# Key-key and key-query products of a chunked delta rule as pairs on two column halves of TensorE, in a new order of the step

## The chip, the cores and the metric

One core of one Trainium2 chip runs the whole kernel. The metric is the device time of one launch in microseconds (us), lower is better. The engines are TensorE (PE; its weight loads are listed apart as PEld), VectorE (DVE), ScalarE (ACT), GpSimd (POOL) and SyncE (SP), which issues most of the DMAs.

## The reference

Everything is float32. Two batches of 2048 tokens with 128 features go through a delta-rule attention with 4 heads and then through a mixture of 8 experts.

```python
q = (x @ Wq).reshape(b, n, H, DK)          # H = 4, DK = 128, DV = 32
k = (x @ Wk).reshape(b, n, H, DK)          # then k /= |k|, q *= DK ** -0.5
v = (x @ Wv).reshape(b, n, H, DV)
beta = sigmoid(x @ Wb)
def step(S, inp):                           # over the n = 2048 tokens
    q_t, k_t, v_t, b_t = inp
    pred = einsum('bhk,bhkv->bhv', k_t, S)
    delta = (v_t - pred) * b_t[..., None]
    S = S + k_t[..., :, None] * delta[..., None, :]
    o_t = einsum('bhk,bhkv->bhv', q_t, S)
    return (S, o_t)
o = o * rsqrt(mean(o * o) + EPS) * norm_w * (g * sigmoid(g))
x = layernorm(x + o @ Wo)
# then: top-2 of 8 experts with a capacity, silu(x @ w1) * (x @ w3) @ w2, weighted sum, layernorm
```

## The kernel before, in words

The attention works on chunks of P = 128 tokens. There are NP = 16 chunks in each of the B = 2 batches, and both batches go through together, so a step of the outer loop handles chunk p of both, in U = 8 units of (batch, head). Keys and queries are never formed. With Mk = Wk Wk^T and Nq = Wk Wq^T for each head, `keys` makes y = Mk x and `queries` makes gq = Nq x, and then two products with x itself give what the chunk needs:

- `key_key(n, b)`: x^T y for the 4 heads of one batch, a matrix of 128 x 512 (4 heads of 128 x 128) in one bank of PSUM. ACT copies it out (`key_key_out`, to `A`). It is symmetric for each head, and what is read of it later is the blocks of 32 x 32 on the diagonal, and of the rest those below the diagonal.
- `key_query(n, b)`: x^T gq, 128 x 512 as well. DVE multiplies it with an upper triangle (`masked`, to `PT`), so that of the lower left quarter of each head nothing is left.

In the profile, the first is the line with `ps<-y,xTs` and the second `ps<-gq,xTs`. A float32 product shows in the trace as two MATMUL records with their weight loads.

The inverse of the chunk's triangular matrix is made in stages, from blocks of 16 (solved on POOL, `solve`) to 32 (`z_32`, `w_32`), to 64 (`z_64`, `w_64`) and to 128 (`z_128`, `w_128`). These are many small products on parts of TensorE's array, and between each two stages stands a copy on DVE or ACT: `z64_copy` (DVE) is between `z_64` and `w_64`, `t64_copy` (DVE) between `w_64` and `z_128`, `z128_copy` (ACT) between `z_128` and `w_128`, `t128_copy` (ACT) between `w_128` and `deltas`. Beside this runs the state: `state_keys`, `keys_read` (DVE), `turn_keys`, `residues` (DVE), `deltas`, `deltas_out` (ACT), `turn_deltas`, `deltas_turned` (ACT), `new_state` and `outputs`. Behind the outputs come `head_sums`, `head_norms` (ACT), `gated_values` and `gated_out` (DVE), `project`, `normalise`, `experts`, `place`, and on POOL `scatter`, which writes rows to the expert slots with four DMA_INDIRECT for each chunk.

All these stages stand in one loop `for p in range(NP + LAST)` on each engine, in an order written out by hand; `at(what, n)` runs a stage if chunk n exists, and chunks at different stages are in work at once. Each engine takes its instructions in program order and waits on semaphores. Three banks of PSUM (0 to 2) go round among the big products: `STEP_FILLS` lists the 10 fills of a step with the chunk that each is for, and fill i takes bank i % 3, so it waits until fill i - 3 has been copied out (`free_bank`). `LV` is the bank of the inverse, `CB` that of the turned tiles, `ZA` the state, `OB` the outputs, `MB` the projection. `apart(eng)` issues a nop ahead of a group. From chunk 5 on, `products` uses a split of both operands into float32r parts, which shows as the lines L684, L685 and L686.

After the attention comes the expert part, in which TensorE, ACT and DVE work on 16 half-experts of 640 slots each; the change doesn't touch it. `keep_on` issues products that nobody reads.

## Time and profile before

| | |
|---|---|
| three runs | 532.18, 538.74, 542.06 us; median 538.74 |
| span of the profiled execution | 539.8 us |
| PE busy | 489.4 us, 91% of the span |
| DVE, ACT, POOL busy | 330.4, 325.2, 325.4 us |
| mean granted clock of TensorE | 0.955 of full speed |

The profiled execution's own time is its span of 539.8 us from first to last instruction, within the three runs. Busy time is the union of an engine's instructions; since the ends of matmuls are modelled and each overlaps the next, a busy PE may still be waiting for a little. The distance from the start of one group to the start of the next is the better measure of what a group costs.

### The profile page before, as it was taken

The numbers are of one execution on the slowest core, as the hardware profiler recorded it, in microseconds if no ns is written. First come the engines' busy times: TensorE is split into PE (matmuls) and PEld (weight loads), VectorE is DVE, ScalarE is ACT, GpSimd is POOL, SyncE is SP. The second block draws the span as 40 slices with busy tenths as digits, with TensorE's granted clock in tenths as the row PEclk, the third lists the DMA queues.
The fourth block names the chain that finished last, engine by engine and source line by source line (L and its number), as shares of the span: only waits on it lengthen the run. The fifth ranks groups of instructions, "written<-read, shape, count | busy, mean of one in ns | idle before, by whom it ended". The sixth has DMA issues, their size and how long they took to land.

```text
span 539.8 us, 18897 instructions
## 1 busy us (share of the span) xinstructions
PE 489.4 (91%) x7053; PEld 403.7 (75%) x7053; DVE 330.4 (61%) x1321; ACT 325.2 (60%) x905; POOL 325.4 (60%) x445
## 2 busy tenths in 40 slices
PE   6979989999999999999997887999999999999910
PEld 4666767767777777676765577999999999999910
DVE  4436558758778686776876762556445565455445
ACT  2645767777768877677664632555555555555454
POOL 3053717867678676786764542376667776767662
PEclk9998999999999999999988878999999999999965
DMA  3358664672554735547183223254536545453367
GB/s 93 31 85 224 215 149 46 94 106 26 73 47 57 101 35 72 49 58 95 24 174 36 32 31 103 36 109 56 109 56 127 110 57 107 60 123 35 30 129 213
DMA packets 154804, 46.09 MB, mean 85 GB/s; under 512 B 107168, under 2 KB 149280, under 8 KB 154720
## 3 DMA queue, kind: packets, MB, share of 16 engines
q1 hardware_dynamic: 132848, 29.86, 28.5%
q0 software_dynamic: 20288, 9.51, 18.9%
q10 hardware_dynamic: 1584, 5.59, 2.7%
q8 instruction: 54, 0.88, 0.7%
q14 instruction: 30, 0.25, 0.1%
HBM read 21.39 MB, written 23.55 MB: 83 GB/s over the span
## 4 chain that ended last, share of the span: by engine, by line
PE 73%; DMA 7%; DVE 7%; issue 6%; ACT 2%; SPq 2%; POOL 1%; ACTq 0%; DVEq 0%; POOLq 0%
PE ps L986 16%; PE ps L997 10%; PE ps L724 5%; PE ps L709 4%; PE ps L681 3%; PE ps L768 2%; PE ps L684 2%; PE ps L758 2%; PE ps L876 2%; PE ps L748 2%; PE ps L850 2%; PE ps L1012 2%; PE ps L780 2%; PE ps L738 2%; PE ps L685 2%
## 5 line engine op out<-in xcount | busy, mean ns | idle before, releaser
L1771 POOL DMA_INDIRECT x_store<-xk,row x80 | 125.1, 1563 | 68.8 <-ACT xk L1258 49.3
L1730 POOL DMA_INDIRECT slots_in<-x,slot x64 | 99.4, 1553 | 29.3 <-issue 17.8
L1589 DVE TENSOR_TENSOR hb<-ps,hs 128x320 f32<-128x320 f32 (+1 forms) x128 | 62.6, 492 | 51.0 <-ACT hs L1250 47.4
L1250 ACT ACTIVATE hs<-ps 128x320 f32<-128x320 f32 (+1 forms) x128 | 55.4, 435 | 34.5 <-PE ps L986 28.9
L986 PE MATMUL ps<-xeTh,w13h 128*128 128x320 f32 x224 | 71.2, 318 | 1.4 <-DVE xeTl L1613 1.0
L986 PE MATMUL ps<-xeTl,w13h 128*128 128x320 f32 x224 | 69.8, 312 | 0.0
L986 PE MATMUL ps<-xeTh,w13l 128*128 128x320 f32 x224 | 69.8, 311 | 0.0
L997 PE MATMUL ps<-w2s,hb 128*128 128x128 f32 x512 | 64.8, 279 | 1.0 <-DVE hb L1589 0.6
L997 PEld LDWEIGHTS ps<-w2s,hb 128*128 128x128 f32 x512 | 59.9, 192 | 3.5 <-DVE hb L1589 1.5
L1712 POOL TENSOR_TENSOR prod<-a,xs 128x28 f32<-128x28 f32 (+11 forms) x120 | 32.7, 272 | 31.5 <-DVE xs L1422 22.8
L1258 ACT ACTIVATE xk<-ps,gs 128x128 f32<-128x128 f32 x80 | 24.2, 365 | 44.5 <-PE ps L1012 34.9
L986 PEld LDWEIGHTS ps<-xeTh,w13h 128*128 128x128 f32 x224 | 42.7, 191 | 1.8 <-issue 1.3
L986 PEld LDWEIGHTS ps<-xeTl,w13h 128*128 128x128 f32 x224 | 42.7, 191 | 0.0
L986 PEld LDWEIGHTS ps<-xeTh,w13l 128*128 128x128 f32 x224 | 42.7, 191 | 0.0
L1744 POOL TENSOR_TENSOR Vk<-V,sq 128x256 f32<-128x256 f32 x16 | 10.7, 671 | 51.4 <-ACT sq L1091 51.3
L1713 POOL TENSOR_TENSOR xs<-xs,prod 128x28 f32<-128x28 f32 (+11 forms) x120 | 33.8, 281 | 9.4
L724 PE MATMUL ps<-gq,xTs 128*128 128x512 f32 x64 | 36.5, 655 | 0.0
L1108 ACT ACTIVATE TT<-x32T 32x256 f32<-32x256 f32 x64 | 26.5, 414 | 15.5 <-DVE x L1364 14.9
L709 PE MATMUL ps<-y,xTs 128*128 128x512 f32 x64 | 34.0, 621 | 1.8 <-ACT eg L1079 1.1
L684 PE MATMUL ps<-xeTh,w13h 128*128 128x256 f32 x99 | 33.3, 337 | 0.0
L1066 ACT ACTIVATE hb<-ps 128x512 f32<-128x512 f32 x32 | 19.1, 597 | 17.9 <-PE ps L709 12.6
L685 PE MATMUL ps<-xeTl,w13h 128*128 128x256 f32 x99 | 27.9, 282 | 0.0
(210 smaller groups left out, 1109.3 us busy)
## 6 DMA issues: line engine op xcount, KB each, us to landing
slots_in<-zeros ACTq DMA_DIRECT2D x10, 520.0 KB, 5.3
xe<-slots_in SPq DMA_DIRECT2D x15, 325.0 KB
w<-w_in SPq DMA_DIRECT2D x8, 448.0 KB
xTs<-xT SPq DMA_DIRECT2D x4, 512.0 KB, 4.9
a_diag<-hb SPq DMA_DIRECT2D x64, 32.0 KB
inv<-xs SPq DMA_DIRECT2D x16, 128.0 KB
xi<-inv SPq DMA_DIRECT2D x16, 128.0 KB
xk<-x SPq DMA_DIRECT2D x8, 256.0 KB, 5.2
```

The source lines that it names most:

```text
L684: mm(to, hi, xhs[:, r], start=True, stop=False)
L685: mm(to, hi, xls[:, r], start=False, stop=False)
L709: mm(ps[:, to, :], xTs[:, b, cols(n)], y[:, n % YR, b].rearrange("p h t -> p (h t)"), start=True, stop=True).then_inc(fill_mm, 1)
L724: mm(ps[:, to, :], xTs[:, b, cols(n)], gq[:, n % 2, b].rearrange("p h t -> p (h t)"), start=True, stop=True).then_inc(fill_mm, 1)
L986: last = mm(ps[:, HB[fill % 5], 0:HALF], w_[:, P * c:P * c + P], x_[:, par, cols], start=(t == 0), stop=(t == 2))
L997: last = mm(result_at(i), hb[:, par, c, P * i:P * i + P], w2s[:, we, c, :], start=(first and c == 0), stop=(stop and c == chunks[-1]), ski ...
L1250: af(hs[to, s % 4, :], ps[src, HB[fill_of(s) % 5], 0:HALF], ACT.Silu).then_inc(hs_ready, 1)
L1589: v.tensor_tensor(hb[to, par, c, HALF * g:HALF * g + HALF], ps[rows_, at, 0:HALF], hs[rows_, s % 4, :], ALU.mult).then_inc(h_ready, 1)
L1712: link(g.tensor_tensor(pr_, bc(a16[r, j + 1:, j], 2, j + 1), bc(xs[r, 0, j, 0:j + 1], 1, m), ALU.mult))
L1713: link(g.tensor_tensor(xs[r, 0, j + 1:, 0:j + 1], xs[r, 0, j + 1:, 0:j + 1], pr_, ALU.subtract))
L1730: g.indirect_dma_start(out=xs_d[:, :], out_offset=bass.IndirectOffsetOnAxis(ap=to, axis=0), in_=x1[:, p % 2, j, k, :], in_offset=None, com ...
L1771: g.indirect_dma_start(out=x1_d[:, :], in_=ye[:, par, i, :], in_offset=None, out_offset=bass.IndirectOffsetOnAxis(ap=row[:, par, i:i + 1], ...
```

## The change

Each 512-column product is cut into two. The array is used as two halves of 64 columns: one half of the output's rows is made with all 512 moving columns, the other half with only the 4 x 64 moving columns of the quarters that are still wanted, so that one quarter of the 128 x 512 result (in each head a block of 64 x 64) is no longer written. For key-key the rows 64 to 127 are whole and the rows 0 to 63 get columns 0 to 63 of each head; for key-query it is the other way about. `key_pair(n, m, b)` issues the products of chunk n (key-key) and of chunk m (key-query) alternately, so that neighbours lie on different column halves. Where only one of the two chunks exists (the first and last steps), only its two products are issued.

The fills' order, and with it the order of the stages on TensorE, ACT and DVE, is another. SP and POOL keep theirs.

```diff
-STEP_FILLS = (("v", 1, 0), ("kk", 1, 0), ("kq", 5, 1), ("g", 4, 0), ("gq", 4, 0), ("gq", 4, 1), ("kk", 1, 1),
-              ("y", 0, 0), ("kq", 4, 0), ("y", 0, 1))
+STEP_FILLS = (("kk", 1, 0), ("kq", 5, 0), ("gq", 4, 0), ("g", 4, 0), ("kk", 1, 1), ("kq", 5, 1), ("gq", 4, 1),
+              ("y", 0, 0), ("y", 0, 1), ("v", 0, 0))
...
+            def key_pair(n, m, b):
+
+                kk, kq = 0 <= n < NP, 0 <= m < NP
+                if kk:
+                    pe.wait_ge(y_free, 2 * n + 2)
+                    to_k = free_bank("kk", n, b)
+                    kT = xTs[:, b, cols(n)]
+                    ys = y[:, n % YR, b]
+                if kq:
+                    pe.wait_ge(gq_out, 2 * m + 2)
+                    to_q = free_bank("kq", m, b)
+                    qT = xTs[:, b, cols(m)]
+                    gs_ = gq[:, m % 2, b]
+                apart(pe)
+                if kk:
+                    mm(ps[64:128, to_k, :], kT[:, 64:128], ys.rearrange("p h t -> p (h t)"), start=True, stop=True)
+                if kq:
+                    mm(ps[0:64, to_q, :], qT[:, 0:64], gs_.rearrange("p h t -> p (h t)"), start=True, stop=True)
+                if kk:
+                    mm(ps[0:64, to_k, :].rearrange("p (h t) -> p h t", h=H)[:, :, 0:64], kT[:, 0:64], ys[:, :, 0:64],
+                       start=True, stop=True).then_inc(fill_mm, 1)
+                if kq:
+                    mm(ps[64:128, to_q, :].rearrange("p (h t) -> p h t", h=H)[:, :, 64:128], qT[:, 64:128],
+                       gs_[:, :, 64:128], start=True, stop=True).then_inc(fill_mm, 1)
...
             for p in range(NP + LAST):
-                at(values, p - 1)
                 at(turn_keys, p - 5)
-                at(key_key, p - 1, 0)
+                at(project, p - 6)
                 at(z_128, p - 5)
-                at(project, p - 6)
...
-                at(key_query, p - 5, 1)
+                key_pair(p - 1, p - 5, 0)
                 at(w_128, p - 5)
+                at(queries, p - 4, 0)
                 at(gate_in, p - 4)
-                at(queries, p - 4, 0)
                 at(deltas, p - 5)
+                key_pair(p - 1, p - 5, 1)
                 at(state_queries, p - 5)
+                at(turn_deltas, p - 5)
                 at(queries, p - 4, 1)
-                at(turn_deltas, p - 5)
-                at(key_key, p - 1, 1)
...
-                at(key_query, p - 4, 0)
+                at(head_sums, p - 5)
+                at(keys, p, 1)
                 at(z_64, p - 4)
                 at(state_keys, p - 4)
-                at(head_sums, p - 5)
-                at(keys, p, 1)
+                at(values, p)
                 at(w_64, p - 4)
```

On TensorE, from `w_64` (`ps<-z,x 32x32`) to `w_128` (`ps<-z,x 64x64`), with `turn_keys` (`ps<-ident,KSt`), `project` (`ps<-wox,og`) and `z_128` (`ps<-TT,hb`) between them, there stands before:

```order
L768 MATMUL ps<-z,x 32x32 x16
L703 MATMUL ps<-wvb,xTs 128x132 x2
L813 MATMUL ps<-ident,KSt 128x128 x2
L709 MATMUL ps<-y,xTs 128x512
L780 MATMUL ps<-TT,hb 64x64 x8
L882 MATMUL ps<-wox,og 128x136 x2
L724 MATMUL ps<-gq,xTs 128x512
L792 MATMUL ps<-z,x 64x64 x8
```

and now, begun two groups earlier at `z_64` (`ps<-x32T,hb`) and `state_keys` (`ps<-y,Zs`):

```order
L771 MATMUL ps<-x32T,hb 32x32 x16
L819 MATMUL ps<-y,Zs 32x128 x8
L703 MATMUL ps<-wvb,xTs 128x132 x2
L781 MATMUL ps<-z,x 32x32 x16
L826 MATMUL ps<-ident,KSt 128x128 x2
L895 MATMUL ps<-wox,og 128x136 x2
L793 MATMUL ps<-TT,hb 64x64 x8
L730 MATMUL ps<-y,xTs 64x512
L732 MATMUL ps<-gq,xTs 64x512
L734 MATMUL ps<-y,xTs 64x4x64
L737 MATMUL ps<-gq,xTs 64x4x64
L805 MATMUL ps<-z,x 64x64 x8
```

The product `ps<-y,xTs` has moved from ahead of `z_128` to behind it, `project` from behind to ahead, and `values` (`ps<-wvb,xTs`) from behind `w_64` to ahead of it; `head_sums` and the second `keys`, which stood between `state_keys` and `w_64`, are now ahead of `z_64`.

On TensorE from `deltas` (`ps<-TT,R`) to `turn_deltas` (`ps<-ident,dT`) and on to `count`, before:

```order
L822 MATMUL ps<-TT,R 32x128 x8
L838 MATMUL ps<-gq,Zs 32x128 x8
L684 MATMUL ps<-xeTh,w13h 128x256
L685 MATMUL ps<-xeTl,w13h 128x256
L686 MATMUL ps<-xeTh,w13l 128x256
...
L829 MATMUL ps<-ident,dT 128x128 x2
L709 MATMUL ps<-y,xTs 128x512
```

and now:

```order
L835 MATMUL ps<-TT,R 32x128 x8
L730 MATMUL ps<-y,xTs 64x512
L732 MATMUL ps<-gq,xTs 64x512
L734 MATMUL ps<-y,xTs 64x4x64
L737 MATMUL ps<-gq,xTs 64x4x64
L851 MATMUL ps<-gq,Zs 32x128 x8
L842 MATMUL ps<-ident,dT 128x128 x2
```

The second pair stands between two groups of the same form (`deltas` and `state_queries`) that were neighbours.

On DVE from the end of `x32_copy` to `x_rest`, before:

```order
L1364 STREAM_TRANSPOSE x<-x32T 128x256
L1405 COPY Zs<-ps 128x256
L1438 TENSOR_TENSOR PT<-ps,upper 128x512
L1371 COPY z<-ps 32x256 x2
L1394 COPY KSt<-ps 128x256
L1445 TENSOR_TENSOR osl<-o,silu 128x256
L1380 TENSOR_SCALAR TT<-ps 32x8x32 x2
L1450 TENSOR_TENSOR og<-osl,orms 128x256
L1389 STREAM_TRANSPOSE x<-TT 32x32 x8
L1400 TENSOR_TENSOR R<-Vk,ps 128x256
L1532 TENSOR_TENSOR xeTl<-xTs,xeTh 128x256
```

and now:

```order
L1374 STREAM_TRANSPOSE x<-x32T 128x256
L1415 COPY Zs<-ps 128x256
L1381 COPY z<-ps 32x256 x2
L1404 COPY KSt<-ps 128x256
L1455 TENSOR_TENSOR osl<-o,silu 128x256
L1460 TENSOR_TENSOR og<-osl,orms 128x256
L1390 TENSOR_SCALAR TT<-ps 32x8x32 x2
L1399 STREAM_TRANSPOSE x<-TT 32x32 x8
L1410 TENSOR_TENSOR R<-Vk,ps 128x256
L1542 TENSOR_TENSOR xeTl<-xTs,xeTh 128x256
L1448 TENSOR_TENSOR PT<-ps,upper 128x512
```

`masked` (`PT<-ps,upper`) left this stretch for one behind `x_rest`, and `gated_out` (`og`) moved ahead of `t64_copy` (`TT<-ps`). On ACT, `z128_copy` now comes ahead of the first `key_key_out`, `x1_rstd` comes behind `gate_out`, and `gate_sigmoid`, `key_norms` and `t_diag` come later, `t_diag` behind `head_norms`.

## Rows read from the trace of the kernel before

**Rows 1.** The page: busy time of TensorE, and the chain that ended last.

```profile
PE 489.4 (91%) x7053; PEld 403.7 (75%) x7053; DVE 330.4 (61%) x1321; ACT 325.2 (60%) x905; POOL 325.4 (60%) x445
...
PE 73%; DMA 7%; DVE 7%; issue 6%; ACT 2%; SPq 2%; POOL 1%; ACTq 0%; DVEq 0%; POOLq 0%
```

**Rows 2.** Busy time in a stretch (start:end, length, engines, granted clock); `turn_keys` from 100 to 240 us.

```profile
140.00:180.00 40.00, 39.55 (x829) 29.53 (x829) 28.63 (x126) 30.33 (x91) 27.52 (x45) 1.00 0.54 68
...
L813 PE MATMUL ps<-ident,KSt x18: 272/272/273, 100.7 to 238.3; 128*128 128x128 f32 x18
```

**Rows 3.** Timeline of TensorE over one step: start, busy us, line, names, forms.

```profile
135.41 0.38 PE L813 MATMUL ps<-ident,KSt 128*128 128x128 f32 x2
135.62 1.02 PE L709 MATMUL ps<-y,xTs 128*128 128x512 f32 x2
136.58 0.68 PE L780 MATMUL ps<-TT,hb 64*64 64x64 f32 x16
137.19 0.73 PE L882 MATMUL ps<-wox,og 128*128 128x136 f32 x4
137.76 1.02 PE L724 MATMUL ps<-gq,xTs 128*128 128x512 f32 x2
138.75 0.68 PE L792 MATMUL ps<-z,x 64*64 64x64 f32 x16
...
140.62 0.64 PE L822 MATMUL ps<-TT,R 128*32 128x128 f32 x16
141.08 0.62 PE L838 MATMUL ps<-gq,Zs 128*32 128x128 f32 x16
...
142.67 1.02 PE L709 MATMUL ps<-y,xTs 128*128 128x512 f32 x2
143.53 0.17 PE L889 MATMUL ps<-M,rest 128*128 128x16 bf16 x1
...
147.46 1.02 PE L724 MATMUL ps<-gq,xTs 128*128 128x512 f32 x2
148.41 0.69 PE L758 MATMUL ps<-x32T,hb 32*32 32x32 f32 x32
149.04 0.77 PE L806 MATMUL ps<-y,Zs 128*32 128x128 f32 x16
...
151.07 0.69 PE L768 MATMUL ps<-z,x 32*32 32x32 f32 x32
151.69 0.72 PE L703 MATMUL ps<-wvb,xTs 128*128 128x132 f32 x4
152.25 0.38 PE L813 MATMUL ps<-ident,KSt 128*128 128x128 f32 x2
```

**Rows 4.** Timeline of the three engines around `z64_copy` and `t64_copy`.

```profile
149.56 0.85 DVE L1371 COPY z<-ps 32x256 f32<-32x256 f32 x2 [0.34 <-PE ps L758]
...
150.43 0.43 DVE L1394 COPY KSt<-ps 128x256 f32<-128x256 f32 x1
150.78 0.41 DVE L1445 TENSOR_TENSOR osl<-o,silu 128x256 f32<-128x256 f32 x1
151.66 1.56 POOL L1730 DMA_INDIRECT slots_in<-x,slot  x1 [0.30 <-issue]
152.97 0.85 DVE L1380 TENSOR_SCALAR TT<-ps 32x256 f32<-32x256 f32 x2 [1.78 <-PE ps L768]
...
153.75 0.40 DVE L1450 TENSOR_TENSOR og<-osl,orms 128x256 f32<-128x256 f32 x1
...
153.92 0.68 PE L780 MATMUL ps<-TT,hb 64*64 64x64 f32 x16 [0.25 <-issue]
```

**Rows 5.** Timeline of TensorE, only what lies in 149.04 to 149.09 us.

```profile
149.04 0.32 PE L806 MATMUL ps<-y,Zs 128*32 128x128 f32 x4
```

**Rows 6.** Two neighbouring stretches near the attention's end, columns as in rows 2.

```profile
251.70:255.10 3.40, 2.35 (x48) 1.27 (x40) 2.49 (x7) 2.00 (x6) 2.79 (x3) 1.00 0.96 65
255.10:258.50 3.40, 3.36 (x22) 2.37 (x22) 3.22 (x17) 0.40 (x2) 2.62 (x3) 0.51 0.82 99
```

More of the change, by code:

```diff
@@ L704, in values @@
                 last.then_inc(fill_mm, 1)
-            def key_key(n, b):
-                pe.wait_ge(y_free, 2 * n + 2)
-                to = free_bank("kk", n, b)
-                mm(ps[:, to, :], xTs[:, b, cols(n)], y[:, n % YR, b].rearrange("p h t -> p (h t)"),
-                   start=True, stop=True).then_inc(fill_mm, 1)
             def queries(n, g):
@@ L719, in queries @@
                 last.then_inc(fill_mm, 1)
-            def key_query(n, b):
-                pe.wait_ge(gq_out, 2 * n + 2)
-                to = free_bank("kq", n, b)
-                mm(ps[:, to, :], xTs[:, b, cols(n)], gq[:, n % 2, b].rearrange("p h t -> p (h t)"),
-                   start=True, stop=True).then_inc(fill_mm, 1)
+            def key_pair(n, m, b):
[21 more added lines that the diff above has]
+                       gs_[:, :, 64:128], start=True, stop=True).then_inc(fill_mm, 1)
             def gate_in(n):
@@ L1189, in _ @@
             for p in range(NP + LAST):
+                at(z128_copy, p - 7)
                 at(key_key_out, p - 3, 0)
-                at(z128_copy, p - 7)
                 at(t128_copy, p - 7)
-                at(x1_rstd, p - 8)
                 at(queries_out, p - 6, 0)
@@ L1196, in _ @@
                 at(gate_out, p - 6)
+                at(x1_rstd, p - 8)
+                at(key_key_out, p - 3, 1)
                 at(deltas_turned, p - 7)
-                at(key_key_out, p - 3, 1)
                 if p == 3:
@@ L1203, in _ @@
                     act.wait_ge(consts_pool, 1)
-                at(softmax, p - 8)
-                at(gate_sigmoid, p - 6)
-                at(key_norms, p - 5)
                 clear(p, 0)
                 at(queries_out, p - 6, 1)
+                at(softmax, p - 8)
                 if p == 6:
@@ L1213, in _ @@
                 at(outputs_out, p - 7)
-                at(t_diag, p - 6)
+                at(gate_sigmoid, p - 6)
+                at(key_norms, p - 5)
                 clear(p, 2)
@@ L1218, in _ @@
                     w_high(0, 0, 0)
-                at(keys_out, p - 2, 0)
                 at(head_norms, p - 7)
@@ L1222, in _ @@
                     w_high(0, 0, 1)
+                at(t_diag, p - 6)
                 clear(p, 3)
+                at(keys_out, p - 2, 0)
                 at(keys_out, p - 2, 1)
@@ L1544, in _ @@
                 at(state_copy, p - 6)
-                at(masked, p - 5, 0)
                 at(z64_copy, p - 5)
@@ L1548, in _ @@
                 at(gated_values, p - 6)
-                at(t64_copy, p - 5)
                 if p - 6 == NP - 1:
@@ L1555, in _ @@
                     w_low(0, 0, 1)
+                at(t64_copy, p - 5)
                 at(x64_turned, p - 5)
@@ L1564, in _ @@
                     solve_first()
+                at(masked, p - 5, 0)
                 at(normalise, p - 6)
-                at(masked, p - 5, 1)
                 at(experts, p - 6)
                 at(inverse_in, p - 4)
+                at(masked, p - 5, 1)
                 at(offsets, p - 6)
```

## The prediction

> **What bounds the kernel now.** I read the page first. TensorE is busy for 91% of the span and carries 73% of the chain that ended last [rows 1]. Then I cut the span into stretches. In the middle of the attention TensorE is busy for 39.55 of 40 us, while DVE has 28.63, ACT 30.33 and POOL 27.52 [rows 2]. So it is TensorE's own stream that sets the step, and the others have a quarter or more to spare. The step's length is the distance of `turn_keys`: 18 records, two a step, from 100.7 to 238.3 us, which is 8 steps in 137.6 us, or 17.2 us a step [rows 2].
>
> A busy row does not say whether TensorE waits a little, so I went down the timeline of one step from start to start [rows 3]. It takes 135.41 to 152.25, 16.84 us, with each group on the heels of the last. The waits show in the step after: its `z_128` starts at 153.92 [rows 4], 1.67 us behind `turn_keys` at 152.25, where the first step has 136.58 - 135.41 = 1.17 [rows 3]. The bare stream is therefore some 16.7 us (my estimate: the 16.84 less small slips), and about 0.5 us of the mean step is waiting.
>
> **The four products.** From start to next start they cost 0.96 (135.62 to 136.58), 0.99 (137.76 to 138.75), 0.86 (142.67 to 143.53) and 0.95 us (147.46 to 148.41), together 3.76 [rows 3]. The third is followed by a group of the same array form, the other three by groups on parts of the array, so 512 columns cost 0.86 and a change of form about 0.10.
>
> The new pair has on each column half one product of 512 and one of 256 moving columns. If the two halves really run side by side, a pair takes 1.5 x 0.86 = 1.29, with the change of form behind it 1.40; two make 2.80. That saves 0.96 a step. Against it stands one more change of form or two: `deltas` and `state_queries` were neighbours of one form (0.46 from start to start) [rows 3], and now the second pair stands between them. I take 0.12. Net 0.84 us a step.
>
> Do the halves run side by side? No 128 x 64 form is in the trace. The nearest row is `state_keys`, 128 x 32 with 128 columns: its 16 records take 0.77 us, one by one at the rate of the big products (0.86 / 2 / 4 = 0.107 each) they would take 1.7. In the first 0.05 us four of its records have begun, and all four lie within 0.32 us [rows 3, 5]. So different column strips, each with a moving operand of its own, do run at once, and the second record of a product does not hold up the first of the next. I take full overlap; the other end of the bound is none at all (below).
>
> **How many steps.** Key-key exists for steps 1 to 16, key-query now for steps 5 to 20. Both meet in 12 steps: 12 x 0.84 = 10.1 us saved. In the other 8 steps one kind is alone, its 512 and 256 columns lie on different halves, and it takes the longer of the two, 0.86, as before; 16 such products each with perhaps 0.1 us for a change of form, less the three in four that had one: 1 us lost.
>
> **The new order.** What counts is how much TensorE work lies between a stage and the one that waits for its copy.
> From `w_64` to `z_128`: before `values` (0.56), `turn_keys` (0.21) and a product (0.96), 1.73 us; now `turn_keys` and `project` (0.57), 0.78 us [rows 3]. In that time DVE must do `t64_copy`, 0.85 us and some 0.1 for the signals [rows 4]. Besides, DVE comes late: from the end of `z_64` it has `z64_copy`, `keys_read`, `gated_values` and now `gated_out` to do, 0.85 + 0.43 + 0.41 + 0.40 = 2.09 us [rows 4], while TensorE passes `state_keys` (0.6 to 0.7), `values` (0.56) and `w_64` (0.62), 1.8 us. So `t64_copy` starts 0.2 us late and `z_128` waits about 0.4 us in every step, where it did not before.
> From `z_64` to `w_64`: before `state_keys`, `head_sums` and `keys`, 151.07 - 149.04 = 2.03 us; now `state_keys` and `values`, 1.2 us, against 0.95 for the copy. Covered, with 0.25 to spare.
> The other covers hold or grow: `deltas` to `turn_deltas` gains the pair, `w_32` to `z_64` goes from 1.5 to about 1.9 us, `z_128` to `w_128` has the pair in place of `project` and a product, 1.4 for 1.56, and needs 0.6.
>
> **The scatter's lock.** In every other step POOL issues its four DMA_INDIRECT while these copies are due. `t64_copy` was ready at 151.76 (151.07 + 0.69), but started at 152.97, 1.31 us into the DMA_INDIRECT of 151.66 [rows 3, 4]. The cost then was 0.4 us at `z_128`, since 1.73 us lay between. The Trainium skill's page "SBUF — State Buffer", section "Who interferes with whom", says that a DVE copy or `tensor_scalar` in a two-port mode and a GpSimd instruction exclude each other for the whole of the one that came first; the late start agrees, and the rule gives no other sum than the row does.
> With the shorter covers I lay the late start anew: if a block of 1.2 us falls on `z64_copy` or on `t64_copy`, some 0.4 us of it show ahead of `w_64` and 0.6 to 1.2 around `project` and `z_128`. I take 1.05 us in such a step, beside 0.4 in the others: 1.45 for two steps, against 2 x 0.5 = 1.0 to 1.1 before. That is 0.2 us a step lost, 12 x 0.2 = 2.4 us. Bounds: nothing waits any more (the old 0.5 goes as well, -6 us), or the full 1.6 in every second step (+6 us).
>
> ACT now has about 13.1 us of work (30.33 / 40 x 17.2) in a step of 16.5 [rows 2]: tight in its order, but not the bound. Last in its step are the copies of `values` and `x_high`, and behind them `z128_copy`, for which `w_128` waits; by the durations it ends just in time. I set that at nothing; if it slips, it costs some 0.3 us a step, 4 us.
>
> **Sum.** 539.8 (the profiled span) - 10.1 + 1 + 2.4 = 533.1. The profiled execution is 1.1 us above the median of 538.74, so against the median 532.
>
> **Rivals.**
> 1. *Clean stream.* The hand-written order hides everything, the old waits included: 15.86 us a step for 17.2, 12 x 1.34 = 16 us, and 1 back: 523. For it: ACT and DVE have room. Against it: the 0.4 us at `z_128` follows from plain sums. 0.17.
> 2. *The clock.* After a stretch in which TensorE worked 2.35 of 3.40 us, without `keys` and `values` (chunks 16 and up don't exist), the granted clock was 0.51, one level (1.2 instead of 2.4 GHz), for the next 3.4 us [rows 6]; that costs 1.7 us. In the steady steps it never fell. The new order brings `z_64`, `state_keys`, `values`, `w_64`, `turn_keys` and the waits together with no big product among them. If it falls in every second step, 6 x 1.7 = 10 us: 542, no change. 0.13, with ACT's slip of 4 us as its lesser form.
> 3. *First in, first out.* The Trainium skill's page "TensorE: Matmul & The Clock Gate", section "The mechanism", states that matmuls start and end strictly in program order. As a mechanism here: each product is two records on one half, and the first record of the next could start no earlier than the second of the last. A pair then goes 2 x 0.43 for the first, 0.43 more for the second, then 0.21 x 3: 1.93 + 0.12 = 2.05, two 4.1 where 3.76 stood; 12 x 0.46 = 5.5, the lone products 16 x 0.3 = 5, and 2.4: 552. Rows 5 speak against it: four records began together. 0.06.
> 4. *No overlap, the slower side.* Full-height halves share a path that 32-wide strips with 128 columns do not show, and a pair costs its columns in series: 3 x 0.86 + 0.1 = 2.7, two 5.4, so +1.7 a step, 12 x 1.7 = 21, and the 16 lone products + 0.43 each, 7: with the rest about 570. It decides as soon as overlap is under a half: a pair over 1.9 us. 0.06.
>
> **The numbers.** The forecast has 0.58, with its own range 526 to 540; the rivals 0.17, 0.13, 0.06 and 0.06. For 8 in 10 the range takes in the clean stream and the clock: 521 to 547. 2% of the median is 10.8 us, about what runs that spread over 10 us can tell from no change. Faster by more (under 528): 0.17 and a little of the forecast, 0.25. Slower (over 549.5): the last two and the worst of the second, 0.14. Within: 0.61.
>
> **What would show it.** In the profile after, the four records of a pair with 512 columns should start two by two, and a pair should take 1.3 to 1.4 us to the next group; if 1.9 or more, rival 3 or 4. `turn_keys` should come every 16.5 us instead of 17.2. `z_128` should show waits of about 0.4 us, and up to 1.2 in every second step. The granted clock between 60 and 250 us should stay 1.00; dips there are rival 2. A `w_128` that waits on ACT would be the slip. I would be wrong altogether if the start or the end of the attention, where latency rules and not the stream, moved by more than 2 us.

## The result and the profile after

| | before | after |
|---|---|---|
| runs, median | 4, 538.65 us (532.18 to 542.06) | 4, 545.33 us (541.52 to 549.23) |
| profiled execution's span | 539.8 us | 547.5 us |
| mean granted clock in it | 0.955 | 0.947 |

The changed kernel takes 1.0236 times as long, 95% interval 1.0185 to 1.0287; the medians differ by 6.7 us (a quotient of 1.0124), where 6.7 us less were forecast. Ratios, here and below, are formed from the fast executions alone and medians from all of them, so a ratio need not be the quotient of two medians, and the profiled execution of e3_cover below was a slow one. Ratio and medians both say slower, but by how much is open by a per cent. The page's busy times and the sums over the middle, of after:

```profile
PE 489.6 (89%) x7181; PEld 402.7 (74%) x7181; DVE 333.8 (61%) x1321; ACT 329.3 (60%) x905; POOL 323.0 (59%) x445
```

TensorE is as busy as before (489.6 for 489.4 us) [rows 1] in a longer span: the columns saved came back as waiting and as time at the lower clock (by the mean granted clock some 58 us of the span for 49). The same stretch and the same 8 steps as in [rows 2], chunks 3 to 11:

```profile
140.00:180.00 40.00, 38.16 (x775) 28.55 (x779) 31.39 (x137) 30.82 (x89) 29.63 (x47) 1.00 0.55 63
...
L826 PE MATMUL ps<-ident,KSt x18: 272/300/330, 104.2 to 243.9; 128*128 128x128 f32 x18
```

TensorE now has 1.84 us unoccupied in 40 where it had 0.45, and a step takes (243.9 - 104.2) / 8 = 17.46 us for 17.20. (The last start is that of a second record; from first record to first record it is 17.44 for 17.19.) By the starts of `turn_keys` the span's 7.7 us divide as follows. Up to chunk 3: 104.2 for 100.7, +3.5. The 8 steps of the middle: +2.1. From there to the last `turn_keys` (313.5 for 304.1 us), 69.6 for 65.8: +3.8. From there to the expert part, 26.3 for 27.6: -1.3. The expert part: -0.4. The forecast had -5.1 in the middle, and outside it only the other four paired steps and the lone products, -1.6 together.

**The pairs work.** The timeline of TensorE through one step, to be held against [rows 3]:

```profile
138.87 0.69 PE L781 MATMUL ps<-z,x 32*32 32x32 f32 x32
139.50 0.44 PE L826 MATMUL ps<-ident,KSt 128*128 128x128 f32 x2
140.22 0.73 PE L895 MATMUL ps<-wox,og 128*128 128x136 f32 x4 [0.28 <-DVE og L1460]
141.14 0.68 PE L793 MATMUL ps<-TT,hb 64*64 64x64 f32 x16 [0.20 <-issue]
141.75 0.64 PE L730 MATMUL ps<-y,xTs 128*64 128x512 f32 x1
141.76 0.64 PE L732 MATMUL ps<-gq,xTs 128*64 128x512 f32 x1
142.23 0.59 PE L730 MATMUL ps<-y,xTs 128*64 128x512 f32 x1
142.24 0.59 PE L732 MATMUL ps<-gq,xTs 128*64 128x512 f32 x1
142.66 0.38 PE L737 MATMUL ps<-gq,xTs 128*64 128x256 f32 x1
...
143.19 0.68 PE L805 MATMUL ps<-z,x 64*64 64x64 f32 x16
...
145.07 0.65 PE L835 MATMUL ps<-TT,R 128*32 128x128 f32 x16
145.73 0.61 PE L730 MATMUL ps<-y,xTs 128*64 128x512 f32 x1
...
147.17 0.65 PE L851 MATMUL ps<-gq,Zs 128*32 128x128 f32 x16
```

The two products of 512 columns (L730, L732) start within 0.01 us of each other, and so do their second records at 142.23: both halves run at once. A pair takes 1.44 us (141.75 to 143.19, and 145.73 to 147.17), forecast 1.40. `deltas` to the pair is 0.66 where `deltas` to its neighbour of one form was 0.46 [rows 3], 0.20 for the forecast's 0.12. So the rows give 3.76 - 2.88 - 0.20 = 0.68 us a step where 0.84 was forecast.

**What waits.** `turn_keys` to `project` takes 0.72 us, and `project` to `z_128` 0.92. With nothing to wait for the first takes 0.27 (shown in the next section) and the second 0.57 by `project`'s own columns [rows 3]; so this step waits 0.45 + 0.35 = 0.80 us, where the forecast had 0.4. Over the 8 steps the two distances are 0.75 and 0.93 in the mean of the starts, 0.84 us of waiting a step. The timeline of DVE and POOL beside it answers to [rows 4]:

```profile
137.77 0.85 DVE L1381 COPY z<-ps 32x256 f32<-32x256 f32 x2 [1.18 <-PE ps L771]
...
138.65 0.42 DVE L1404 COPY KSt<-ps 128x256 f32<-128x256 f32 x1
...
138.99 0.41 DVE L1455 TENSOR_TENSOR osl<-o,silu 128x256 f32<-128x256 f32 x1
139.01 0.86 POOL L1753 TENSOR_TENSOR Vk<-V,sq 128x256 f32<-128x256 f32 x1
139.44 0.72 DVE L1460 TENSOR_TENSOR og<-osl,orms 128x256 f32<-128x256 f32 x1
139.84 0.90 POOL L1747 TENSOR_TENSOR silu<-G,sg 128x256 f32<-128x256 f32 x1
...
140.19 0.85 DVE L1390 TENSOR_SCALAR TT<-ps 32x256 f32<-32x256 f32 x2
```

DVE runs through `z64_copy`, `keys_read`, `gated_values`, `gated_out` and `t64_copy` without a gap, and both waits of TensorE hang on that one queue: `project` starts 0.06 us behind `gated_out`'s end, `z_128` 0.10 behind `t64_copy`'s. `gated_out` took 0.72 us, not 0.40 [rows 4], while POOL's two products, themselves longer than usual, ran. And DVE had stood idle for 1.18 us before `z64_copy`. This step is one of two kinds. In every second step POOL's two products lie beside `gated_values` and `gated_out`, and these take 0.3 to 0.9 us longer together (`gated_out` 0.72 here and 0.83 once, `gated_values` 0.86 to 0.95 in the other three); the waiting at the two places is 1.06 us in the mean of these four. In the four steps between, both take 0.41 or 0.42 us and the waiting is still 0.62: that much is the order of the queue alone. In these four steps `z64_copy` starts late beside a DMA_INDIRECT, and the two distances ahead of `w_64` are 0.40 us longer than in the others.

**The two ends.** The granted clock (the column of 1.00 or 0.50), in stretches near the start, at 246.6 and near the attention's end, each with the stretch ahead of it:

```profile
38.40:41.80 3.40, 1.79 (x70) 1.34 (x70) 0.89 (x3) 0.00 (x0) 2.63 (x9) 1.00 0.60 140
41.80:55.50 13.70, 13.32 (x197) 8.99 (x197) 8.22 (x28) 6.31 (x17) 1.98 (x5) 0.50 0.73 182
...
243.20:246.60 3.40, 2.44 (x56) 1.92 (x58) 3.27 (x12) 2.77 (x8) 3.02 (x3) 1.00 0.32 77
246.60:250.00 3.40, 3.40 (x24) 1.42 (x24) 1.30 (x6) 0.98 (x2) 3.01 (x2) 0.51 1.07 132
...
284.20:287.60 3.40, 0.78 (x43) 0.66 (x44) 1.06 (x3) 0.73 (x2) 3.05 (x2) 1.00 1.08 180
287.60:301.30 13.70, 13.60 (x245) 9.28 (x232) 8.16 (x34) 6.78 (x21) 7.59 (x6) 0.50 0.73 135
```

TensorE ran at its lower level (1.2 GHz) for 13.7 us twice. Before, the fall near the start lasted 3.4 us, and from chunk 11 to the expert part there were four, of 3.4, 3.4, 3.4 and 10.2 us. In that same part there are now three, of 3.4, 13.7 and 3.4 us: 20.5 us at the lower level as before. But up to the last `turn_keys` it is 17.1 us for 10.2, and behind it 3.4 for 10.2, which is much of the +3.8 and of the -1.3. Each long one stands behind a long wait of `z_32` for the block inverses. These are TensorE's waits at the start (34 to 41 us), and DVE's and POOL's near the end (255 to 300 us):

```profile
PE ps L751 <- DVE xh L1358: 2.5, 1, 2.5
...
POOL Vk L1753 <- ACT sq L1102: 10.3, 2, 6.6
DVE x32T L1357 <- DMA xi<-inv: 4.2, 1, 4.2
```

Near the end the chain reads: ACT comes to `key_norms` late, POOL's product `Vk` waits for it (10.3 us here, 3.1 before), the `solve` behind it in POOL's queue ends at 278.9 us where it ended at 269.6 (3.7 us later against chunk 11's `turn_keys`), the inverses come late, and TensorE waits from 284.67 to 287.30.

### The profile page after: what moved, and what is told of

It is laid out like the page before. It is cut to its first block, busy times and chain, and to the rows that moved or that the text cites. A ratio compares the mean times of both kernels' runs of the same rounds, so it can differ in the third digit from the quotient of the medians.

```text
span 547.5 us, 19153 instructions
## 1 busy us (share of the span) xinstructions
PE 489.6 (89%) x7181; PEld 402.7 (74%) x7181; DVE 333.8 (61%) x1321; ACT 329.3 (60%) x905; POOL 323.0 (59%) x445
## 4 chain that ended last, share of the span: by engine, by line
PE 71%; DVE 8%; DMA 8%; issue 6%; SPq 3%; ACT 2%; POOL 1%; ACTq 0%; DVEq 0%; POOLq 0%
PE ps L997 15%; PE ps L1008 10%; PE ps L730 5%; PE ps L681 3%; PE ps L771 3%; PE ps L684 2%; PE ps L737 2%; PE ps L793 2%; PE ps L895 2%; PE ps L685 2%; PE ps L761 2%; PE ps L686 2%; PE ps L889 2%; PE ps L805 2%; PE ps L863 2%
## 5 line engine op out<-in xcount | busy, mean ns | idle before, releaser
L1739 POOL DMA_INDIRECT slots_in<-x,slot x64 | 98.3, 1536 | 25.2 <-issue 16.8
L1753 POOL TENSOR_TENSOR Vk<-V,sq 128x256 f32<-128x256 f32 x16 | 10.1, 630 | 66.4 <-ACT sq L1102 66.3
L732 PE MATMUL ps<-gq,xTs 128*64 128x512 f32 x64 | 37.8, 675 | 0.0
L730 PE MATMUL ps<-y,xTs 128*64 128x512 f32 x64 | 35.0, 638 | 1.5 <-ACT y L1063 1.0
L1448 DVE TENSOR_TENSOR PT<-ps,upper 128x512 f32<-128x512 f32 x32 | 22.0, 687 | 17.7 <-PE ps L734 12.8
```

The costliest lines, as they stand in the source:

```text
L730: mm(ps[64:128, to_k, :], kT[:, 64:128], ys.rearrange("p h t -> p (h t)"), start=True, stop=True)
L732: mm(ps[0:64, to_q, :], qT[:, 0:64], gs_.rearrange("p h t -> p (h t)"), start=True, stop=True)
L1739: g.indirect_dma_start(out=xs_d[:, :], out_offset=bass.IndirectOffsetOnAxis(ap=to, axis=0), in_=x1[:, p % 2, j, k, :], in_offset=None, com ...
```

## The experiments

All ratios are to the kernel before on the same chip. "Step" is the mean of the 8 steps of chunks 3 to 11 in the profiled execution, as above; the median of before was 534.1 to 536.1 us on these chips.

| label | median us | ratio (95%) | step us | chunk 3 at us |
|---|---|---|---|---|
| before | 538.65 | | 17.20 | 100.7 |
| after | 545.33 | 1.0236 (1.0185 to 1.0287) | 17.46 | 104.2 |
| e1_whole | 553.16 | 1.0318 (1.0165 to 1.0471) | 18.00 | 106.6 |
| e2_gated | 535.40 | 1.0045 (0.9937 to 1.0154) | 16.83 | 102.2 |
| e3_cover | 541.00 | 1.0090 (0.9916 to 1.0265) | 17.10 | 102.1 |
| e4_both | 537.34 | 1.0115 (1.0014 to 1.0216) | 16.84 | 103.6 |
| e5_keep | 539.77 | 1.0085 (1.0051 to 1.0119) | 17.23 | 100.7 |
| e6_gated_keep | 534.81 | 1.0004 (0.9962 to 1.0046) | 16.73 | 100.4 |
| e7_gate | 537.29 | 1.0056 (1.0017 to 1.0095) | 16.96 | 100.6 |
| e8_halves | 541.22 | 1.0121 (1.0077 to 1.0165) | 17.79 | 101.6 |
| e9_norms | 544.76 | 1.0156 (1.0082 to 1.0230) | 17.40 | 108.2 |
| e10_all | 537.55 | 1.0016 (0.9975 to 1.0057) | 17.34 | 99.8 |
| e11_before_look | 532.96, one run | | 17.16 | 102.7 |
| e12_whole_gated | 556.95 | 1.0350 (1.0215 to 1.0485) | 18.75 | 105.2 |

### The new order alone: e1_whole

```diff
-mm(ps[64:128, to_k, :], kT[:, 64:128], ys.rearrange("p h t -> p (h t)"), start=True, stop=True)
-mm(ps[0:64, to_q, :], qT[:, 0:64], gs_.rearrange("p h t -> p (h t)"), start=True, stop=True)
...
+mm(ps[:, to_k, :], kT, ys.rearrange("p h t -> p (h t)"), start=True, stop=True).then_inc(fill_mm, 1)
+mm(ps[:, to_q, :], qT, gs_.rearrange("p h t -> p (h t)"), start=True, stop=True).then_inc(fill_mm, 1)
```

> The changed kernel's order with whole products: each key-key and key-query product is one product of 128 x 512 again, and all else, the order on every engine too, is as in the changed kernel. The dead quarters are computed as in the kernel before. Theory W (the new order brings waits of 0.9 us or more around turn_keys, project and z_128, and the pairs only pay for them): the pairs lie outside the stretch that waits, so without them the step grows by 3.5 - 2.9 = 0.6 to 0.9 us, 12 steps: 552 to 556 us, and the waits at project and z_128 stay. Theory H (the halved form itself is what costs): 532 to 540, at or under the kernel before. Theory C (the clock falls because halves work the array less): the granted clock between 40 and 56 us comes back to one short fall as before, 541 to 545.

The new order with whole products is the slowest but one, 18.00 us a step: the order alone costs 0.80 us a step, and in it the pairs give 0.54 of that back. Two whole products and the next change of form stand there as

```profile
145.12 1.12 PE L730 MATMUL ps<-y,xTs 128*128 128x512 f32 x2
...
146.08 1.02 PE L732 MATMUL ps<-gq,xTs 128*128 128x512 f32 x2
147.04 0.68 PE L799 MATMUL ps<-z,x 64*64 64x64 f32 x16
```

from 145.12 to 147.04, 1.92 us where a pair of halves takes 1.44, so two pairs save 0.96 a step by this row (0.89 in the mean of the 8 steps). Not all of it arrives: from `turn_keys` to `project` takes 0.57 in the mean here and 0.75 in the changed kernel, and there POOL's products lengthen DVE's two by at most 0.3 us.

### The halves alone: e8_halves

```diff
 def key_key(n, b):
-    mm(ps[:, to, :], xTs[:, b, cols(n)], y[:, n % YR, b].rearrange("p h t -> p (h t)"),
+    apart(pe)
+    mm(ps[64:128, to, :], kT[:, 64:128], ys.rearrange("p h t -> p (h t)"), start=True, stop=True)
+    mm(ps[0:64, to, :].rearrange("p (h t) -> p h t", h=H)[:, :, 0:64], kT[:, 0:64], ys[:, :, 0:64],
```

`key_query` is cut likewise, and all stands in the order of the kernel before.

> The kernel before, in its own order, with each key-key and key-query product cut into its two halves (64 x 512 and 64 x 4 x 64 on different column halves), but not paired: the change's form without its order. The quarter is left out, but nothing runs in its place. By the pair's 1.44 us in the trace after, a lone product takes its 512 columns, 0.86, and up to 0.1 more for changes of form: the same as before, up to +3 us (535 to 542 beside 538.7). If the halved form as such lowered the clock or ran slower (theory H), it would show here as 5 us or more, and the granted clock would dip between 60 and 250 us.

```profile
137.71 0.38 PE L819 MATMUL ps<-ident,KSt 128*128 128x128 f32 x2
138.02 0.64 PE L711 MATMUL ps<-y,xTs 128*64 128x512 f32 x1
138.02 0.65 PE L712 MATMUL ps<-y,xTs 128*64 128x256 f32 x2
...
139.02 0.68 PE L786 MATMUL ps<-TT,hb 64*64 64x64 f32 x16
```

A halved product on its own takes 1.00 us (138.02 to 139.02) and comes 0.31 behind `turn_keys`, for 0.96 and 0.21 of a whole one [rows 3]: 0.14 worse, four times a step 0.56, and the step is longer by 0.59. Without a partner the halves save nothing and pay the change of form. If the 16 lone products of the changed kernel cost the same, they take 2.2 us (an estimate from this row), forecast 1.

### DVE's queue: e2_gated, and more cover: e3_cover, e4_both

The order on DVE, in e2_gated:

```diff
 at(state_copy, p - 6)
-at(z64_copy, p - 5)
-at(keys_read, p - 5)
 at(gated_values, p - 6)
 at(gated_out, p - 6)
+at(z64_copy, p - 5)
+at(keys_read, p - 5)
 at(t64_copy, p - 5)
```

> The changed kernel with gated_values and gated_out ahead of z64_copy on DVE, where DVE now idles for 1.2 us; TensorE's and ACT's orders as in the changed kernel. Theory W with DVE's queue as the cause: og is then ready before project asks, and t64_copy starts as soon as w_64 is done; the wait ahead of project (0.5 us) goes and that ahead of z_128 becomes 0.2 to 0.4. Saves 0.5 to 0.7 us a step, 16 steps: 534 to 538. If the cover on TensorE is too short whatever DVE does, the waits only move to z_128 and it stays at 543 to 546.

```profile
134.15 0.51 DVE L1460 TENSOR_TENSOR og<-osl,orms 128x256 f32<-128x256 f32 x1 [0.52 <-ACT orms L1155]
...
134.57 0.84 DVE L1381 COPY z<-ps 32x256 f32<-32x256 f32 x2
...
136.19 0.44 PE L826 MATMUL ps<-ident,KSt 128*128 128x128 f32 x2
...
136.31 0.85 DVE L1390 TENSOR_SCALAR TT<-ps 32x256 f32<-32x256 f32 x2 [0.44 <-PE ps L781]
136.46 0.63 PE L895 MATMUL ps<-wox,og 128*128 128x136 f32 x4
...
137.26 0.68 PE L793 MATMUL ps<-TT,hb 64*64 64x64 f32 x16 [0.17 <-issue]
```

(Two timelines of one step, by start.) `gated_out` now runs in the time in which DVE stood idle. `project` follows `turn_keys` at 0.27 us instead of 0.72, `z_128` follows `project` at 0.80 instead of 0.92, and `t64_copy` waits for `w_64` (0.44) instead of TensorE for it. The step falls by 0.63 us to 16.83, and the ratio to the kernel before from 1.0236 to 1.0045, the intervals apart. The queue of DVE held the middle up; this is shown, and e6_gated_keep below, held against e5_keep, shows it once more (17.23 to 16.73).

e3_cover puts the second `keys` between `state_keys` and `w_64` again and `values` behind `w_64`, DVE's order untouched; e4_both has both edits. The order on TensorE in e3_cover:

```diff
 at(head_sums, p - 5)
-at(keys, p, 1)
 at(z_64, p - 4)
 at(state_keys, p - 4)
-at(values, p)
+at(keys, p, 1)
 at(w_64, p - 4)
+at(values, p)
```

> The changed kernel with TensorE's order mended at one place: z_64, state_keys, second keys, w_64, values instead of second keys, z_64, state_keys, values, w_64. So 0.99 us of keys lie between z_64 and w_64 and values between w_64 and z_128. Theory W: both waits (0.9 us together) go, the step comes to 16.5, 12 to 16 steps: 528 to 533 us. Theory C: the clock falls as in the changed kernel and it gets back at most 3 us of it: 541 or more. Theory H: no change, 545.

> Both edits of the last two runs. Theory W: little is left to gain from DVE once TensorE's stretch is long enough, so 526 to 532, within 2 us of the run with TensorE's order alone. If DVE's queue holds something else up (the products' masks, the experts), it comes out 3 us or more apart from it.

More cover on TensorE gives 0.36 us a step, and on top of the DVE edit nothing (16.84 for 16.83). They are two cures of one wait.

### The start: e5_keep

```diff
 if p == 4:
-    keep_on(22)
+    keep_on(36)
```

`keep_on` issues products that nobody reads; now they last until the first inverse is there.

> The changed kernel with keep_on(36) instead of keep_on(22) in step 4, so that TensorE has something to do in the 2.8 us in which it waits for the first inverse (36.3 to 39.1 us); nothing else is edited. Theory C1 (the long fall of the clock near the start, 13.7 us at half speed from 41.8 us, comes from that wait, and costs some 4 us): the fall gets shorter or goes, turn_keys of the second and third step come 3 to 5 us earlier, 541 us. Theory C2 (it comes from the small products and waits in steps 4 and 5 themselves): the fall stays where it is, 545.

```profile
39.74 1.17 PE L912 MATMUL ps<-ident 128*128 128x128 f32 x9
40.84 0.73 PE L751 MATMUL ps<-xh,hb 32*32 32x16 f32 x64
...
39.00:53.00 14.00, 13.05 (x302) 9.63 (x300) 8.63 (x29) 7.23 (x19) 4.93 (x16) 1.00 0.77 187
```

(A timeline at the start, then busy time in a stretch.) `z_32` follows the idle products at once, and the granted clock stays 1.00 where it had been 0.50. Chunk 3 comes at 100.7 us, 3.5 earlier and where it was before the change; the ratio falls from 1.0236 to 1.0085, and the intervals are apart. So the 3.5 us of the start came from the wait and the fall behind it. The other profiles bear this out: in the four kernels with `keep_on(36)` there is no fall near the start and chunk 3 comes at 99.8 to 100.7 us, and in the seven of the new order without it a fall of 6.8 to 17.1 us stands there and chunk 3 comes at 102.1 to 108.2.

The line is worth less than the ratios say. The two profiled spans differ by 9.3 us, of which 3.5 lie up to chunk 3, 1.9 in the 8 steps, 0.6 from there to the last `turn_keys` and 3.2 behind it, and nothing was edited in the last three. The middle in particular: it has the changed kernel's order and a step of 17.23 us where the changed kernel's profile has 17.46, so two profiles of one order differ by 0.23 us a step, nearly as much as the new order seemed to lose on the old. What is firm is that the 0.64 us a step that were forecast did not come. At the other end the line does nothing: there `z_32` still waits 3.0 us, and the clock was 0.50 for 17.1 us from 279.1 on.

### Both cures, and their next waits: e6_gated_keep, e7_gate

e6_gated_keep is e2_gated with e5_keep's line.

> DVE's order of e2_gated and the longer keep_on of e5_keep. By theory C1 some 4 us less than e2_gated, 531. By C2 the same as e2_gated. In the middle the step stays 16.8 us either way.

It ties with the kernel before, 1.0004 (0.9962 to 1.0046), over 12 runs: the best version found, and no gain. Its step is 16.73, 0.47 under before, its chunk 3 at 100.4. Near the end it loses what it won: from chunk 11's `turn_keys` to the last takes 301.9 - 234.2 = 67.7 us for 65.8, with the clock at 0.50 for 10.2 us from 279.3.

e7_gate is e6_gated_keep with `gate_in` between `project` and `z_128`, to cover the 0.2 us left there (its fill goes first in `STEP_FILLS`, and `gate_out` first on ACT).

```diff
 at(project, p - 6)
+at(gate_in, p - 4)
 at(z_128, p - 5)
```

> As e6_gated_keep, and gate_in moved on TensorE from behind queries to between project and z_128 (its fill to the head of the step's fills, gate_out on ACT to behind z128_copy). Theory W says that z_128 still waits some 0.4 us for t64_copy in e2_gated, since too little lies between w_64 and z_128, and gate_in (0.43 us) fills just that: the step goes from 16.8 to 16.4 us, and the time 5 to 6 us under e6_gated_keep. If the wait only moves (to the pair, whose bank now waits for values, or to w_128 behind gate_out on ACT), the step stays at 16.8.

```profile
PE ps L730 <- ACT V L1072: 4.5, 9, 0.7
```

The wait moved and grew: now the pair waits 0.5 us in every step for the bank that ACT's copy of `values` sets free, and the step is 16.96.

### The other end: e9_norms, e10_all, and before again: e11_before_look

On ACT, in e9_norms:

```diff
 at(outputs_out, p - 7)
+at(gate_sigmoid, p - 6)
+at(key_norms, p - 5)
...
-at(gate_sigmoid, p - 6)
-at(key_norms, p - 5)
```

> The changed kernel with gate_sigmoid and key_norms on ACT back where they stood in the kernel before, ahead of the second queries_out; nothing else is edited. POOL waits for key_norms (66.3 us in all in the profile after, 51.3 before) and then sends four DMA_INDIRECT before it may begin the next solve. Theory P (the wait of 2.7 us ahead of z_32 at 284.5 us, and the fall of the clock for 13.7 us right behind it, come from POOL being late with the last solve): that wait goes, the attention's last steps get 4 to 6 us shorter, in all 540 against 545. The middle step stays 17.4. Rival: the last solve is late for want of its blocks from SP's queue, or by the shorter step; then the wait stays.

POOL's wait for `key_norms` falls from 66.3 to 49.8 us over the kernel, TensorE's wait ahead of that late `z_32` from 2.6 to under 1 us, and the way from chunk 11 to the last `turn_keys` from 69.6 to 65.7 us, as before the change. So the wait ahead of `z_32` went with ACT's order. That this order by itself cost the 3.8 us is not shown: e1_whole, e2_gated and e4_both have the changed kernel's order on ACT, no wait of 0.8 us or more ahead of that `z_32`, and take 63.4, 65.4 and 61.9 us for the same way (e11_before_look, the kernel before again, takes 62.0, 3.8 less than its first profile). The new order makes the late inverse possible, and it shows in some of its versions. And the time hardly moved: 1.0156, an interval that overlaps with the changed kernel's. In its profile the clock fell in the middle instead, at 91.0 and at 196.9 us, each time behind a stretch with waits at `w_64` or `z_128`, and its chunk 3 comes at 108.2 us, 4 later than the changed kernel's:

```profile
193.50:196.90 3.40, 2.38 (x52) 1.92 (x53) 2.66 (x12) 3.18 (x9) 2.79 (x3) 0.99 0.94 105
196.90:200.30 3.40, 3.40 (x21) 1.29 (x18) 2.46 (x12) 0.52 (x2) 1.35 (x4) 0.50 0.31 30
```

e10_all has all three edits (e2_gated, e5_keep, e9_norms).

> DVE's order of e2_gated, keep_on(36) of e5_keep and ACT's order of e9_norms together. By theories W, C1 and P each takes its part: the middle step 16.7 us, no fall of the clock near 42 us, no wait of 2 us or more ahead of z_32 near the end: 529 to 533 where the kernel before has 534 to 538, a ratio of 0.985 to 0.995. If the parts only hand the wait on, it is the same as e6_gated_keep, ratio 1.00.

> The kernel before once more, for a second profile of it. Its times have ranged from 527 to 544 us on the chips used. All theories expect the middle step at 17.2 us within 0.1; what differs between its runs should lie in the clock's falls at the start and end of the attention (49 us at half speed in the first profile) and in the expert part.

With all three the ratio is 1.0016 (0.9975 to 1.0057), no better than without the ACT edit; its step is 17.34 and it too has a fall in the middle, at 153.5. With ACT's order of e9_norms the DVE edit moves the step by only 0.06 us (17.40 to 17.34). The second profile of the kernel before has the same step as the first (17.16 and 17.20), but chunk 3 comes 2.0 us later and the way from chunk 11 to the last `turn_keys` is 3.8 us shorter, with the falls elsewhere. That is how far one profile can be trusted here: the step to 0.04 us in this pair and 0.23 in that of the changed kernel and e5_keep, the ends to 2 to 4 us, the place of the falls not.

### Are the parts additive? e12_whole_gated

This is e1_whole with the DVE edit of e2_gated.

> The new order with whole products of e1_whole and DVE's order of e2_gated; the dead quarters are computed again. It tells what the pairs are worth once DVE's queue no longer holds TensorE up. The rows of TensorE give 3.76 us for four whole products before and 2.88 + 0.2 for two pairs with their changes of form: 0.68 us a step. Theory W: the step is 16.81 + 0.68 = 17.5 us, 12 steps make 8 us, so some 544 beside 535.4. If the pairs only lengthen other waits, the step is under 17.2.

The edit that saved 0.63 us a step with pairs costs 0.75 with whole products. TensorE, DVE and POOL at one `t64_copy`, the next `t64_copy`, and the stretches around the clock's fall at 127.3 us:

```profile
104.86 1.60 POOL L1733 DMA_INDIRECT slots_in<-x,slot  x1
...
105.43 0.63 PE L889 MATMUL ps<-wox,og 128*128 128x136 f32 x4
106.47 0.85 DVE L1384 TENSOR_SCALAR TT<-ps 32x256 f32<-32x256 f32 x2 [1.71 <-PE ps L775]
...
124.98 1.56 POOL L1733 DMA_INDIRECT slots_in<-x,slot  x1 [0.30 <-issue]
125.55 0.85 DVE L1384 TENSOR_SCALAR TT<-ps 32x256 f32<-32x256 f32 x2 [1.50 <-PE ps L775]
...
123.90:127.30 3.40, 2.17 (x55) 1.89 (x51) 1.84 (x11) 2.63 (x9) 2.79 (x3) 1.00 0.85 192
127.30:130.70 3.40, 3.40 (x5) 0.86 (x4) 2.23 (x9) 0.98 (x2) 1.81 (x5) 0.50 0.42 39
```

`w_64` had ended at 105.22 and DVE was idle, but `t64_copy` started at 106.47, some 1.2 us late, at the end of POOL's DMA_INDIRECT (104.86 + 1.60). The next one was 1.1 us late, but started at 125.55, inside the DMA_INDIRECT from 124.98 to 126.54. Two such waits of `z_128`, 1.2 us ending at 126.50 and 1.4 us ending at 219.17, were followed by a fall of the clock; two others, of 1.4 us ending at 107.42 and 1.25 us ending at 182.63, were not. The two falls of 3.4 us cost up to 1.7 us each (half of their time, an estimate), which is 0.4 of the 0.75 us a step. Between 100 and 240 us `z_128` waits 6.3 us here. In the changed kernel `t64_copy` was never held up so, and `z64_copy` by 0.5 to 0.7 us in every second step. There a `t64_copy` even ran inside a DMA_INDIRECT, right behind another instruction of DVE:

```profile
104.55 1.60 POOL L1739 DMA_INDIRECT slots_in<-x,slot  x1 [0.16 <-issue]
...
105.17 0.85 DVE L1390 TENSOR_SCALAR TT<-ps 32x256 f32<-32x256 f32 x2
```

An earlier or later DVE queue meets another part of POOL's scatter, so the worth of an edit depends on all the others. That the scatter's place decides is argued from these rows; a kernel without the scatter wasn't tried.

## Why the prediction was wrong

The direction was wrong (532 forecast, 545.3 measured, within 521 to 547). The mechanism of the pair was right. Two steps of the prediction failed: the sum for the new order, 0.2 us a step net where the profile has 0.83 us more waiting a step, and the ends, for which it had no term and where the profiled execution lost 3.5 and 3.8 us. That the time still lies in the range is the width of the range, not the reasoning.

**The pair: right in mechanism, a little small in size.** Full overlap, 1.44 us for 1.40. The change of form cost 0.20 for 0.12, so by the rows 0.68 us a step in place of 0.84: 8.2 us for 10.1 in 12 steps. The lone products cost 2.2 for 1, if e8_halves holds for them; by the forecast's own terms (16 products at 0.1, less the three in four that had a change of form) the 1 should have been 0.4.

**The new order: the step that failed most.** The forecast exchanged 0.5 us of old waiting a step for 0.4 in one step and 1.05 in the next, 0.2 us net. Take as waiting what each distance between two groups has over its smallest in the 8 steps, with 0.27 and 0.57 for `turn_keys` and `project` (an estimate). Then the kernel before waits 0.65 us a step and the changed one 1.48: 0.83 net. The bare stream is 0.58 us shorter, and 0.83 - 0.58 is the +0.25 measured. The 1.48 are 0.84 around `project` and `z_128`, 0.21 ahead of `w_64`, 0.09 at `deltas` and 0.34 in small parts elsewhere. The first two the forecast had at 0.73 together (the mean of 0.4 and 1.05); for the others it had no term.

"So `t64_copy` starts 0.2 us late and `z_128` waits about 0.4 us in every step." The place was right; in the step shown the wait is 0.80 us, on both sides of `project`. By the forecast's own sum, with `z64_copy` at 137.77 and the durations of before, `t64_copy` would have ended at 140.71 and `z_128` been some 0.5 late; nearly all the rest is `gated_out` at 0.72 instead of 0.40. In the four steps without such lengthening the wait is 0.62. I took the durations from a place where POOL's products didn't run beside them. And I read only how late DVE's queue ends, not that DVE stands idle ahead of it. With `gated_out` out of that queue (e2_gated) the two distances are 0.27 and 0.89 in the mean, 0.32 us of waiting: near the 0.4 of the forecast.

**The scatter's lock: right in size by luck.** In every second step the forecast had 1.05 us at the two places, for a `t64_copy` or `z64_copy` blocked by a DMA_INDIRECT, and 1.06 was measured. But in those steps it is POOL's two products that lengthen DVE's; the late `z64_copy` falls into the other steps, where it costs 0.40 us ahead of `w_64` (the "some 0.4" of the forecast). In e1_whole, where the products are whole as before, the order costs 0.80 us a step against 0.2 forecast, 9.6 us in 12 steps for 2.4. The forecast's outer bound was 6. It treated the position of the scatter as given; e2_gated and e12_whole_gated show that one edit of DVE is worth +0.63 or -0.75 with it.

The prediction says that the late start agrees with the Trainium skill's page "SBUF — State Buffer", section "Who interferes with whom". The traces agree only in part. The copy at 106.47 of e12_whole_gated started when the DMA_INDIRECT was over, but that at 152.97 [rows 4] started 0.25 us before its end, that at 125.55 in the midst of one, and that at 105.17 of the changed kernel ran inside one without a wait. The same section says that a DVE instruction with at most one input in SBUF, outside the two-port modes, does not contend with GpSimd; `t64_copy` reads PSUM, and no run here shows its mode. So the late starts beside the scatter are seen, and their rule is open.

**The ends: an assumption of nothing.** The forecast named it ("if the start or the end of the attention, where latency rules and not the stream, moved by more than 2 us") and gave it no term. The ends moved by 3.5 and 3.8 us. What stands there could be read beforehand: `key_norms` moved back on ACT, POOL's `Vk` and with it the next `solve` wait for it, and the start and end have no stream over it. e5_keep takes the first back, and that cause is shown. e9_norms takes the wait of the second away, but the 3.8 us are no more than what two profiles of the kernel before differ by, so its price is not shown.

**The rivals.** The time is nearest to rival 2's (542), but by other means: in the changed kernel's profile the clock fell once in the steady steps, at 246.6, not in every second step, and for longer behind the two long waits at the ends. In e9_norms, e10_all and e12_whole_gated it did fall in the middle, behind waits in the stretch that rival 2 named. The clean stream (1) needed DVE to have room where it matters. Rival 3, first in, first out, is refuted: a pair takes 1.44 us, not 1.9 or more. The Trainium skill's page "TensorE: Matmul & The Clock Gate", section "The mechanism", says that matmuls start and end strictly in program order. Here L732's first record starts at 141.76, beside L730's first and 0.47 ahead of L730's second, so between two column halves the trace does not bear it out for a product of two records. Rival 4, no overlap, falls by the same rows. ACT's slip did not show: `w_128` is 1.44 behind the pair's start, on its heels. Its price came elsewhere, at `key_norms`.

**What stays open.** By the means of the starts over the 8 steps the middle's +0.25 is, each group up to the start of the next: the four products, from 4.00 to 2.92, -1.09; `turn_keys` and `project`, from 0.80 to 1.68, +0.88; `deltas`, from 0.46 to 0.69, +0.23; `state_keys` and `values`, from 1.15 to 1.43, +0.28; `turn_deltas`, from 0.36 to 0.20, -0.16; `head_sums`, -0.10; all others together +0.21. Nothing is left over, but which of it belongs to the order and which to one execution is open, since e5_keep's middle has 17.23. How much of the order's cost is the lock and how much the queue was not told apart, and neither was what would be needed for the end of e6_gated_keep to keep its 0.47 us a step.

## What to carry to other kernels

A saving on the busiest engine is worth only what the queues around it can follow: after shortening TensorE's stream, add up the queue of the engine that serves it from its first idle moment to the copy that is waited for, and put what is ready early into that idle time. Judge a new order with the computation unchanged before the two are combined; here the order alone cost 0.80 us a step and the cheaper products gave back 0.54. And look at start and end by themselves: a wait of 2.5 us where 1.0 us had stood cost 3.5 us, since the clock fell behind it for longer, and one line that kept TensorE occupied took these 3.5 us back. Profile a kernel more than once before a few us at its ends are given a cause.

## What the runs showed of the hardware

- Two 64-column halves of the array run float32 products of 512 and 256 moving columns side by side: 1.44 us a pair, against 1.92 for two whole products of 512; a halved product without a partner takes 1.00 us, and 0.1 us more ahead of it.
- The clock fell to its lower level behind waits, and the length of the fall varied: 13.7 us behind a wait of 2.5 us, 3.4 us behind waits of 0.8 + 0.2 (246.6 us in the changed kernel) and of 1.2 us (127.3 in e12_whole_gated), none behind waits of 1.4 and 1.25 us there (107.42, 182.63). Idle products in place of the first wait kept the granted clock at 1.00 (e5_keep).
- A DVE product of 128 x 256 took 0.72 us beside two POOL products of the same shape, and 0.40 without; POOL's took 0.86 and 0.90 there, 0.61 and 0.72 in e2_gated, where DVE's two ran earlier.
- DVE copies out of PSUM that were ready beside POOL's DMA_INDIRECT started late: 1.2 us in e12_whole_gated, at the DMA_INDIRECT's end (106.47) or inside the next one (125.55). One right behind another DVE instruction ran inside a DMA_INDIRECT without a wait (105.17 in the changed kernel).
